# First group's attention moved forward, and VectorE given part of the last expert passes

## What is computed

```python
x = x + 0.5 * ffn_fp4(layernorm(x))        # two inputs rounded block by block (16 values) to FP4
x = x + mamba2(layernorm(x))               # 2 state-space layers: 256 channels, 16 states, a scan over time
x = x + 0.5 * ffn_fp4(layernorm(x))
x = x + 0.5 * experts(layernorm(x))        # 8 experts: relu(x W1 + b1) W2 + b2, hidden 512
x = x + attention(layernorm(layernorm(x))) # 16 heads of 8, causal, relative bias, softmax
x = x + 0.5 * experts(layernorm(x))        # the same 8 experts a second time

def experts(x):
    p = sigmoid(x @ Wg + bg); w = p * (p > 0.5)      # one weight per token and expert
    h = relu(einsum('td,edh->eth', x, W1) + b1)
    y = einsum('eth,ehd->etd', h, W2) + b2
    return einsum('te,etd->td', w, y)
```

## Time and profile before

| | before |
|---|---|
| median of 3 runs | 2610.5 us (2609.67 to 2610.94) |
| profiled execution, its own time | 2610.92 us |
| its span, first to last instruction | 2609.1 us |
| PE, PE weight load, VectorE, ScalarE, GpSimd busy | 92%, 64%, 72%, 60%, 52% |
| mean granted TensorE clock | 0.957 of full |

### The profile page before, as it was taken

How to read it: one execution, slowest core, us unless ns; L and a number is a source line. 1 busy time by engine, 2 the same in 40 slices (tenths; PEclk the granted TensorE clock), 3 DMA queues, 4 the chain that set the end, 5 groups by cost and what they waited for, 6 DMA issues and landing times.

```text
span 2609.1 us, 40448 instructions
## 1 busy us (share of the span) xinstructions
PE 2392.5 (92%) x14313; PEld 1680.7 (64%) x14313; DVE 1866.3 (72%) x3817; ACT 1559.5 (60%) x3377; POOL 1368.1 (52%) x1227
## 2 busy tenths in 40 slices
PE   7999997997898999889898989999898999988988
PEld 7878884685565666656565656666575656666675
DVE  5879797789587978698687968797879777322220
ACT  1424435543686558664886668665876685566654
POOL 1466483947373856558373847476564737212001
PEclk9999998998899999999899999999999999989999
DMA  4123131312220222112230222121311422100100
GB/s 152 56 76 108 48 97 37 101 46 85 79 90 31 82 86 93 37 63 76 90 90 30 89 86 86 41 79 65 105 54 58 126 60 71 34 20 1 49 5 5
DMA packets 97640, 175.30 MB, mean 67 GB/s; under 512 B 11957, under 2 KB 23133, under 8 KB 95646
## 3 DMA queue, kind: packets, MB, share of 16 engines
q1 hardware_dynamic: 97438, 172.71, 21.6%
HBM read 157.44 MB, written 15.23 MB: 66 GB/s over the span
## 4 chain that ended last, share of the span: by engine, by line
PE 66%; DVE 12%; ACT 11%; POOL 6%; issue 5%; DMA 0%; SPq 0%; POOLq 0%; DVEq 0%; ACTq 0%
PE c_bank L912 15%; PE c_bank L920 14%; PE c_bank L1351 8%; PE a_bank L758 7%; PE a_bank L748 3%; PE b_bank L1060 3%; DVE hst L706 2%; POOL prod_c L829 2%; PE a_bank L727 2%; PE b_bank L580 2%; PE b_bank L1050 1%; ACT weighted_y L955 1%; POOL prod_c L834 1%; PE b_bank L1099 1%; PE b_bank L561 1%
## 5 line engine op out<-in xcount | busy, mean ns | idle before, releaser
L829 POOL TENSOR_TENSOR prod_c<-hst,prod_c 128x512 f32<-128x512 f32 x512 | 670.9, 1318 | 382.0 <-DVE hst L706 362.4
L706 DVE TENSOR_TENSOR_SCAN hst<-dA,a_bank 128x512 f32<-128x512 f32 x512 | 621.1, 1213 | 9.6
L920 PEld LDWEIGHTS c_bank<-w,hid 128*128 128x128 f32 x4096 | 506.8, 196 | 75.7 <-ACT hid L947 38.6
L912 PE MATMUL c_bank<-c_xT,w 128*128 128x512 f32 x1024 | 534.4, 628 | 21.7 <-ACT hid L947 12.1
L920 PE MATMUL c_bank<-w,hid 128*128 128x128 f32 x4096 | 523.0, 280 | 7.6 <-ACT hid L947 7.5
L818 ACT ACTIVATE dA<-delta,a_neg 128x510 f32<-128x510 f32 x512 | 365.2, 719 | 269.1 <-DVE hst L706 260.4
L1351 PEld LDWEIGHTS c_bank<-ident 128*128 128x128 f32 x3632 | 439.1, 194 | 36.1 <-issue 27.2
L1351 PE MATMUL c_bank<-ident 128*128 128x128 f32 x3632 | 445.3, 277 | 1.7 <-ACT weighted_y L955 1.7
L947 ACT ACTIVATE hid<-c_bank,b 128x512 f32<-128x512 f32 x512 | 349.6, 687 | 150.8 <-PE c_bank L912 148.8
L971 POOL TENSOR_TENSOR xs<-xs,weighted_y 128x512 f32<-128x512 f32 x128 | 166.2, 1298 | 426.3 <-ACT weighted_y L955 424.7
L700 DVE TENSOR_TENSOR a_bank<-du,a_bank 128x512 f32<-128x512 f32 x512 | 348.5, 681 | 37.1 <-PE a_bank L748 35.6
(11 more groups left out here) (177 smaller groups left out, 2814.5 us busy)
## 6 DMA issues: line engine op xcount, KB each, us to landing
prod_c<-c_rows SPq DMA_DIRECT2D x512, 256.0 KB, 3.2
q_and_k<-qk_rows SPq DMA_DIRECT2D x64, 192.0 KB
qk_rows<-att_buf SPq DMA_DIRECT2D x40, 256.0 KB, 2.6
w<-in_w SPq DMA_DIRECT2D x2, 2048.0 KB
xs<-in_x SPq DMA_DIRECT2D x8, 256.0 KB, 6.7
bias<-skew SPq DMA_DIRECT2D x1, 2048.0 KB, 8.0
qk_rows<-b_xn SPq DMA_DIRECT2D x8, 256.0 KB, 3.0
out_dram<-xs SPq DMA_DIRECT2D x8, 256.0 KB, 2.4
```

The source lines that it names most:

```text
L706: nc.vector.tensor_tensor_scan(hst[:, s % RS, :], dA[:, s % RA, :], b_bank, 0.0, ALU.mult, ALU.add).then_inc(M.h.sem, 1)
L829: nc.gpsimd.tensor_tensor(prod[:, s % RP, :], hst[:, s % RS, :], cring[:, s % RC, :], ALU.mult).then_inc(M.pp.sem, 1)
L912: nc.tensor.matmul(S.bank[up_bank(e, c)][:, :], w1[:, e, c * 128:(c + 1) * 128], S.xT[:, :], start=True, stop=True).then_inc(M.up.sem, 1)
L920: ins = nc.tensor.matmul(S.bank[down_bank(f)][:, t * D:(t + 1) * D], hid[:, f % 2, j, t * 128:(t + 1) * 128], w2[:, f, j, :], start=(j == ...
```

## The change

- `moe_order` and `b_order` are built by a loop: group 0's attention comes before the feed-forwards (1,1) and (0,3), and its second expert pass before pass (0,1). From group 1 on the order is as before.
- In the last three passes (`first_late` = 13: (0,7), (1,6), (1,7)) ScalarE rectifies chunks 0 and 2 of an expert and VectorE chunks 1 and 3; VectorE adds the four weighted tiles of a down product straight from PSUM to x, where ScalarE scaled and GpSimd added. Waits on `relu`, `wy` and `acc` become waits on `even`, `odd` and `lacc`.
- In the attention of groups 6 and 7 VectorE copies the transposed exponentials to `pT` instead of ScalarE, and `y_end` moves within its queue.
- All five order strings are new. Warm-ups are issued only until the first of the three late passes has ended, since `moe.wy` isn't signalled in them. In the strings there are 1853 warm-ups (before: 1816): 1836 up to lane a's last piece (before 1719), 17 behind it (before 97). At that piece the lanes b and c have gone as far as before (686 and 816 pieces of PE).

```diff
-        moe_order = [(0, 0)]
-        b_order = [(0, 0), (0, 1), (1, 0), (0, 2)]
-        for g in range(1, GROUPS):
-            moe_order += [(0, g), (1, g - 1)]
-            b_order += [(1, g), (0, g + 2), (2, g - 1)]
+        prompt = 1
+        moe_order, b_order = [], [(0, 0), (0, 1)]
+        for g in range(GROUPS):
+            moe_order.append((0, g))
+            b_order += [(1, g), (0, g + 2)]
+            if g < prompt:
+                b_order.append((2, g))
+                moe_order.append((1, g))
+            elif g > prompt:
+                b_order.append((2, g - 1))
+                moe_order.append((1, g - 1))
...
+        first_late = len(moe_order) - 3
...
 (moe_dve)
+            for e in range(EXPERTS + 1 if L.g >= first_late else 0):
+                for c in range(1, HC, 2):
+                    if e < EXPERTS:
+                        dve.wait_ge(M.up.sem, L.at(M.up, e * HC + c + 1))
+                        if e >= 2 and c == 1:
+                            dve.wait_ge(M.down.sem, L.at(M.down, e - 1))
+                        nc.vector.tensor_scalar(hid[:, e % 2, c, :], S.bank[up_bank(e, c)][:, :], b1[:, e, c:c + 1], 0.0,
+                                                ALU.add, ALU.max).then_inc(M.odd.sem, 1)
+                        yield
+                if e >= 1:
...
+                    for t in range(TT):
+                        ins = nc.vector.scalar_tensor_tensor(out=x[:, t, :], in0=S.bank[down_bank(f)][:, t * D:(t + 1) * D],
+                                                             scalar=gw[:, t, f:f + 1], in1=x[:, t, :], op0=ALU.mult, op1=ALU.add)
...
 (moe_pe, the second up of an expert)
-                            pe.wait_ge(M.wy.sem, L.at(M.wy, e - 1))
+                            if L.g < first_late:
+                                pe.wait_ge(M.wy.sem, L.at(M.wy, e - 1))
+                            else:
+                                pe.wait_ge(M.lacc.sem, late(L, M.lacc, e - 1))
...
 (attn_dve)
-                if r >= 7 and r % 4 == 3:
-                    yield from y_end(r // 4 - 1)
+                if L.g < GROUPS - 2:
+                    if r >= 7 and r % 4 == 3:
+                        yield from y_end(r // 4 - 1)
+                elif r >= 2:
+                    if r >= 6 and r % 4 == 2:
+                        yield from y_end(r // 4 - 1)
+                    yield from copied(dve, L, S, M, r - 2)
...
 (warm_pe)
                 assert L.passes is not None
+                assert L.passes <= first_late
```

More of the change, by code:

```diff
@@ L48 @@
[L48 to L57, removed]
@@ L416, in build, with late, wait_experts, wait_relu @@
         ffn_order = [o for o in b_order if o[0] < 2]
+        first_late = len(moe_order) - 3
+        def late(L, signal, k):
+            assert 1 <= k <= signal.per and L.g >= first_late
+            return signal.per * (L.g - first_late) + k
+        def wait_experts(eng, second, g):
+            i = moe_order.index((second, g))
+            if i < first_late:
+                eng.wait_ge(moe.acc.sem, moe.acc.per * (i + 1))
+            else:
+                eng.wait_ge(moe.lacc.sem, moe.lacc.per * (i - first_late + 1))
+        def wait_relu(eng, L, M, n):
+            if L.g < first_late:
+                eng.wait_ge(M.relu.sem, L.at(M.relu, n))
+            else:
+                eng.wait_ge(M.even.sem, late(L, M.even, (n + 1) // 2))
+                if n > 1:
+                    eng.wait_ge(M.odd.sem, late(L, M.odd, n // 2))
         def stats_dve(dve, L, S, x, done):
@@ L872, in moe_dve @@
             yield
+            for e in range(EXPERTS + 1 if L.g >= first_late else 0):
[8 more added lines that the diff above has]
+                if e >= 1:
+                    f = e - 1
+                    dve.wait_ge(M.down.sem, L.at(M.down, f + 1))
+                    if f == 0:
+                        dve.wait_ge(M.xb2.sem, L.at(M.xb2, 1))
+                    else:
+                        dve.wait_ge(M.lacc.sem, late(L, M.lacc, f))
+                    for t in range(TT):
+                        ins = nc.vector.scalar_tensor_tensor(out=x[:, t, :], in0=S.bank[down_bank(f)][:, t * D:(t + 1) * D],
+                                                             scalar=gw[:, t, f:f + 1], in1=x[:, t, :], op0=ALU.mult, op1=ALU.add)
+                        if t == TT - 1:
+                            ins.then_inc(M.lacc.sem, 1)
+                        else:
+                            ins.then_inc(L.sem, L.one())
+                    yield
         def up_bank(e, c):
@@ L942, in moe_act @@
                 for c in range(HC):
-                    if e < EXPERTS:
+                    if e < EXPERTS and (L.g < first_late or c % 2 == 0):
                         act.wait_ge(M.up.sem, L.at(M.up, e * HC + c + 1))
@@ L964, in moe_pool @@
             yield from rstd_pool(pool, L, S, M.norm.stats, M.norm.rstd)
-            for f in range(EXPERTS):
+            for f in range(EXPERTS if L.g < first_late else 0):
                 pool.wait_ge(M.wy.sem, L.at(M.wy, f + 1))
@@ L1009, in y_end @@
                 yield
-            for r in range(NH):
+            for r in range(NH + 2 if L.g >= GROUPS - 2 else NH):
                 h = r % HEADS
+                if r >= NH:
+                    yield from copied(dve, L, S, M, r - 2)
+                    continue
                 dve.wait_ge(M.s.sem, L.at(M.s, r // 2 + 1))
```

167 lines of the change are left out of this document (96 added, 71 removed).

## The result

| | before | after |
|---|---|---|
| median | 2610.5 us (2609.67 to 2611.37, 7 runs) | 2620.26 us (2617.86 to 2623.6, 7 runs) |
| ratio, 95% interval | | 1.0035 [1.0025, 1.0045] |
| profiled execution, span | 2610.92, 2609.1 | 2620.26, 2618.1 |
| lane a's last layer starts its out projection | 2203.7 | 2219.1 |
| from there to the end | 405.4 | 399.0 |

The prediction was 2603.0 (2589 to 2617), so the result is on the other side of before and outside the range.

What follows compares the result with a forecast made beforehand. The mamba part was taken as bound by chains across VectorE, GpSimd and PE, the 405.4 us behind it by PE. Terms of -8.0 us behind and 0 in the mamba part took 2610.9 to 2602.9, called 2603 (2589 to 2617).

Steps and rivals of the forecast that it cites:

- The tail: Everything behind the mamba part, 405.4 us before: the gains and clock costs there were to sum to -8.0 us.
- Mixed experts: Experts in passes (0,7) and (1,6) beside attention: PE's waits shrink, 1.1 us off 11.38 each, -12.7 us in all.
- Bare experts: Pass (1,7) and first experts of (1,6): VectorE's four additions replace scalings, 0.25 us less for 11 experts, -2.8 us.
- The end, -1.5: Kernel's end: after the last down, four additions replace the scalings and GpSimd's addition, -1.5 us.
- Missing warm-ups: Attention 7's end and the last pass's start run at half clock without 74 warm-ups: net +5.5 and +4 us.
- clock: Rival: all 9.5 us of attention 7's remaining PE work doubles, the last pass loses 7; 2610 us, chance 0.12.
- holds: Rival: full clock in attention 7's end, or its cost hidden behind other engines; 9.5 us less, 2593.5, chance 0.20.
- Attention 0 moved: Mamba layers 5 and 6: attention one layer earlier, together 274 us against 277.5, -4 us (bounds +5, -10).
- Warm-ups in the mamba part: 117 more warm-ups, 26 us of PE: four to six late steps in each of layers 1 to 3, +4 us.
- Its sign of being wrong: In the mamba part: lane a's end 15 us later, with the first four layers longer by 5 each.
- warm-ups on the path: Rival: the 117 mamba warm-ups delay each step behind them, up to 26 us; at 21, 2620 us, chance 0.13.
- From layer 7 on nothing: Mamba layers from 7 on: strings as full of warm-ups as before, so no cost from them.

Runs made afterwards that it cites:

- late passes alone: Kernel before with its group order and strings up to lane a's last piece, the changed kernel's late passes and strings behind it; 2605.62 us.
- late_warm: The late passes alone, with 74 warm-ups put back where attention 7 runs alone and ahead of the last pass; 2599.85 us.
- after_thin: Changed kernel with 137 warm-ups fewer in mamba layers 1 to 4, back to before's count in each; 2612.06 us.
- after_warm: Changed kernel with before's 74 warm-ups put back into attention 7's end and ahead of the last pass; 2613.7 us.
- after_mid: Changed kernel with before's strings from the end of layer 7 to lane a's last piece; 2615.23 us.
- first group of experiments: The two halves of the change run separately, and the changed kernel with warm-ups put back and thinned; the kernel before took 2611.07 us beside them.

## Why the prediction was wrong, point by point

The tail was right to 1.6 us (-6.4 for -8.0). What failed is the sum of the mamba part, -4 + 4 = 0, which measured +15.4: the new strings of layers 8 to 16, put at nothing, cost 6.5; the moved attention, put at -4, gave +1.0; the warm-ups of the first layers, put at +4, cost 7.9. Each is told below at its place.

- **Mixed experts, 1.1 us each**: 0.79. Pass (0,7) from head to head 108.4 to 101.9, -6.5 for the -7.7 of seven experts (in the late passes alone 103.2, -5.2). Pass (1,6) with the clock held 128.1 to 122.0, -6.1; the forecast had -5.0 for its mixed experts. The mechanism is right, PE is the bound as said.
- **Bare experts, -0.25 each**: +0.12. The 0.25 rested on four additions of 0.29 that overlap down to 0.9 us, against 1.14 for the scalings. One takes 0.344 (the row of 0.29 had the shape, not the instruction), four take 1.13, and nothing is won. The rectification's 0.684, a floor by the nearest row, was 0.750.
- **The end, -1.5**: from the start of PE's last run of downs to the store 9.85 us before, 8.50 in `late_warm`: -1.35.
- **Missing warm-ups, +5.5 and +4.0**: +4.3 and +1.7 (the late passes alone against those with warm-ups). The clock is low over the stretch, as forecast: it falls between 2509 and 2510 us, behind 3 us in which PE was busy 0.88 us. A cost of 16.5 ("clock") or none ("holds") is out. The Trainium skill's rule on gaps between bursts (TensorE: Matmul & The Clock Gate, "HAM oscillation — how this bites in real kernels") prices a stretch at the low clock at half of its length, by which 44 us would cost 22, an estimate. The trace agrees with the low clock, 0.50 from first to last, but not with that price: the stretch cost 6.1 us. PE was busy 27.5 of the 44 us, half of which would be 13.8; that the chain over three engines hid the rest is inferred.
- **Attention 0 moved, -4**: layers 5 and 6 took 263.4 us, much less than the 274 named, but layers 3 and 4 took 12.6 us more even at before's warm-ups (`after_thin`), with 4 more PE pieces of lane b in their strings, and layer 7 took 2.6 to 4.4 us more. With before's warm-ups in layers 1 to 4, lane a reaches layer 7's end at 950.7 or 948.4 for 949.7: nothing, so this step failed by 4 to 5 us. Layers 5 to 7 have 70 warm-ups fewer than before, 55 of them in layer 7, whose clock is 0.90 for 0.98; what the move gives apart from that stays open.
- **Warm-ups in the mamba part, +4 of 26: this step was sized at half.** It saw that VectorE's u had no slack and that PE was busy 96.6 of 97.1 us in layer 2, and still counted four to six places a layer instead of all steps; and it priced layers 1 to 3 and left out layer 4's 49. Its sign of being wrong, lane a 15 us later with the first four layers longer by 5 each, came true in part: lane a was 15.4 us later, and the four layers were longer by 0.2, 1.8, 12.8 and 3.7. Put back to the old counts the warm-ups gave 8.2 us, and in before's own queues 137 more cost 21. The rival "warm-ups on the path" was right in before's queues, but in the changed kernel 8.2 of 30.6 us is far from its 21 of 26: that the time is its 2620 is luck, since two other terms made up the difference.
- **From layer 7 on nothing: this step failed, and is the largest miss.** The sum of the warm-ups was compared, 358 for 363, and neither their places nor the order of the rest. The new strings of layers 8 to 16 cost 6.5 us in the trace, and 5.0 us came back when they were undone. Whether their order or their 50 warm-ups more cost it is open. The forecast had named this part's new order, but only as a spread of 7 us to either side.

The sum by experiment, each from single traces: -6.4 (tail), +7.9 (warm-ups of layers 1 to 4: lane a at layer 7's end 958.6 against 950.7), +1.0 (moved attention and the rest of layers 1 to 7), +6.5 (strings of layers 8 to 16), together +9.0: span 2609.1 to 2618.1. In the trace of `after_warm`, whose strings are the same up to the tail, layer 7 ends at 954.4, so the second and third term are uncertain by some 4 us. The last is 6.5 to 9.3 in the three traces with the new strings (1260.5, 1261.2 and, in `after_thin`, 1263.3 for 1254.0).

## What to carry to other kernels

Filler in an in-order queue has a price curve with a kink: free up to the wait that it fills, then a part of its length for each: in before's first four layers a third (layer 2) to 85% (layer 4), in the changed kernel's a quarter on the whole. Before adding any, read the idle time ahead of the real instructions between; where it is a few tenths in a whole layer, as in layer 2 here, the filler is at the edge. When the order is rewritten, compare the filler layer by layer, not in sum. And a gain at the end of a kernel can be measured only with the queues elsewhere unchanged: the late passes and their warm-ups, spliced onto the old order, beat both kernels (2599.85 us, 0.41% under before).

## What was not expected of the hardware

- On VectorE a 128x512 PSUM rectification with bias takes 750 ns, where the copy with a factor of the earlier trace rows took 684 and ScalarE's 688; a 128x128 weighted addition from PSUM 344 ns, where a custom 128x128 maximum took 285; four of them in a row 1.13 us, as the four scalings of ScalarE.
- Executions of one kernel differ by some us, and the longer ones are those with the lower granted clock: in `after_mid` 2611.04 us at 0.954 and 2619.76 us at 0.949. The changed kernel's seven spread over 5.7 us and the 11 of `after_mid` over 8.7; those of before over 1.7 in seven, but over 5.9 in the 31 run beside the first group of experiments. A single trace can be 3 us off the median, so differences of 3 us between two traces are not read as effects.
